# Fused mask, scale and maximum in three attentions, paired reciprocals, and half of the turned probabilities copied by VectorE

## The chip, the cores and the metric

The kernel runs on one core of a Trainium2 chip. The metric is the device time of one execution in microseconds. The core has five engines that run side by side and wait for each other by semaphores: TensorE (PE: matmuls and transposes, with its weight loads as PEld), VectorE (DVE), ScalarE (ACT), GpSimd (POOL) and SyncE (SP, which issues transfers).

## The reference

The reference is a decoder of four layers on x, 8 rows of 256 tokens and 256 features. Each layer has a sequence mixer, an attention over a context and a feed-forward part. The change touches the softmax attentions:

```
_L1_attn   16 heads of 16; relu(q k^T) * R_hat, causal, softmax(scores / 4), times v      (tag L1a)
_L1_xattn  16 heads of 16; score = where(mask == 0, -1e20, q k^T); softmax(score / 4), v  (tag L1x)
_L2_xattn  one head of 256; q k^T / 16 + mask * -1e9; softmax, times v                    (tag L2x)
_L3_xattn  8 heads of 64, 512 keys (256 context + 256 latents); q k^T / 64, masked;
           softmax, times v, Wo, layernorm                                                (tag L3x)
```

## The kernel before, in words

One function, `softmax_attention`, makes L1a, L1x and L3x; `layer2_xattn` makes L2x. Everything is float32. The work of the first is cut into items: 16 per row of the batch, 128 in all. An item is the scores of 128 partitions against W keys: 384 in L1a (a causal tile of 128 and one of 256), two heads' 256 in L1x, 512 keys of one head in L3x. G items are one step: 4 in L1a and L1x (`twins == 2`), 2 in L3x (`twins == 1`). So there are 32 steps in L1a and L1x (4 per row) and 64 in L3x (8 per row). S is the number of softmax rows in an item, 2 in L1a and L1x and 1 in L3x.

An item goes through these stations: TensorE makes the scores in a PSUM bank (`scores`, L1136); VectorE scales them and adds the mask into SBUF (`scale_mask`, L1358; L1355 in L1a) and takes the negated maximum (`maximum`, L1370; L1368 in L1a); ScalarE makes the exponential with that maximum as bias and the sum of the row (`exponent`, L1250; the sum comes out by a second instruction of that line); VectorE inverts the sum (`reciprocal`, L1377); GpSimd multiplies the probabilities by it (L1296; L1300 in L1a); TensorE turns them (`transposes`, L1147) into one of two PSUM banks; ScalarE (L1259) or VectorE (L1346) copies them to SBUF (`take_turned`), after which the bank is free again; TensorE multiplies the values with them (`weigh`, L1169). `by_dve` says which items VectorE copies: the last of each step in L1a and L1x, none in L3x.

Nothing is planned at run time. Each engine's program is written out in order, and each runs its instructions in that order. On TensorE, with LA = 2, step u of the loop is

```
transposes of the first half of step u-2's items
[at the first step of a row: output projection of the row before, L1121]
weigh(u-3)
projections q, k or v of the next row (L1089, L1103, L1110), in most steps
scores(u+1)
transposes of the second half of step u-2's items
```

`weigh` waits until the last two items of its step are copied. VectorE goes item by item: `reciprocal(g - RLAG)` with RLAG = 4 in L1a and L1x and 3 in L3x, then the maximum of item g, with `scale_mask` one item ahead. In L3x `scale_mask(g+1)` of a step's first item stands at the end of the step before, so it is the first thing that VectorE does when new scores are there. Once a row it has also the work of the row's end: in L3x `spread` (statistics of the output, L1388 to L1393) and `output` (normalisation and residual, L1400 to L1413), both ahead of `reciprocal`, in the second and third step after the output projection. ScalarE does, item by item, the exponential and the copy of a turned item.

`layer2_xattn` runs 16 items of 128x256 in the same manner, two per row: copy of the context slice and mask (L1571, L1573), scores (L1508), scale and mask (L1578), maximum (L1581), exponential (L1543), transposes (L1516), copy (L1550), values (L1524), and then reciprocal, scaling and residual on VectorE (L1561 to L1565).

Of the kernel before, what the change touches and what calls it, by code (L numbers as in the profile page):

```python
# [20 lines left out]
B, T, D = 8, 256, 256  # L21
# [12 lines left out]
ACT = mybir.ActivationFunctionType  # L34
ALU = mybir.AluOpType
AX = mybir.AxisListType
# [849 lines left out]
def softmax_attention(c, tag, H, rows, MQ, KT, DV, kind, scale, norm=None):  # L886
# [13 lines left out]
    nc, w = c.nc, c.dram  # L900
    NK, C = KT * P, H * DV
    causal = kind == "decay"
    twins = 2 if rows == 16 else 1
# [4 lines left out]
    G = P // (rows * twins)  # L908
# [5 lines left out]
    n, S = len(items), len(items[0][1])  # L914
# [8 lines left out]
        UNITS = [[("q", 0)], [("q", 1)], [("k", 0)], [], [("v", 0)], [("k", 1)], [("v", 1)], []]  # L923
    in_order = [unit for kind_ in "qkv" for step_units in UNITS for unit in step_units if unit[0] == kind_]
    units_at = lambda u: [(r_, *unit) for r_ in [u // PER_ROW + 1] if r_ < ROWS for unit in UNITS[u % PER_ROW]]
    by_dve = lambda key: twins == 2 and key[0] == "p" and key[1] % G == G - 1

    turned = [(kind_, 0, i) for kind_, i in in_order if kind_ != "k"]
    for u in range(steps + LA):
# [4 lines left out]
    with ExitStack() as stack:  # L934
# [102 lines left out]
        with nc.Fori(0, B // ROWS) as turn:  # L1037
            with nc.Block() as block:
# [169 lines left out]
                def _(act):  # L1208
# [34 lines left out]
                    def exponent(g):  # L1243

                        r, i = divmod(g, n)
                        if g >= NP:
                            act.wait_ge(t_filled, turn_index[("p", g - NP)] + 1)
                        act.wait_ge(sig("max"), g + 1)
                        for e, (t, at, nk) in enumerate(items[i][1]):
                            nc.scalar.activation(p_sb[g % NP][:, at:at + nk], s_sb[g % NSB][:, at:at + nk], ACT.Exp,  # L1250
                                                 bias=nmax[r % 2][:, i, e:e + 1],
                                                 accum_out=rsum[r % 2][:, i, e:e + 1]).then_inc(sig("exp"), 1)

                    def take_turned(j):
# [33 lines left out]
                @block.gpsimd  # L1288
                def _(pool):
                    for r in range(ROWS):  # L1290
                        for i, (h, segs) in enumerate(items):
                            g = r * n + i
                            pool.wait_ge(sig("reciprocal"), g + 1)
                            if len({nk for _, _, nk in segs}) == 1:
                                both = p_sb[g % NP][:].rearrange("p (e s) -> p e s", e=S)
                                last = nc.gpsimd.tensor_tensor(both, both, rsum[r % 2][:, i, :].unsqueeze(2).to_broadcast([P, S, NK]), ALU.mult)  # L1296
                            else:
                                for e, (t, at, nk) in enumerate(segs):
                                    one = p_sb[g % NP][:, at:at + nk]
                                    last = nc.gpsimd.tensor_tensor(one, one, rsum[r % 2][:, i, e:e + 1].to_broadcast([P, nk]), ALU.mult)  # L1300
                            last.then_inc(sig("divided"), 1)

                @block.vector
                def _(dve):
# [8 lines left out]
                    def hide(r):  # L1313

                        if kind == "decay":
                            return
                        dve.wait_ge(sig(f"mask{r % 2}"), 16 * (r // 2 + 1))
                        b_, m_ = bias[r % 2], mask[r % 2]
                        if kind == "pairs":
                            vec.tensor_scalar(b_[:], m_[:], 0.0, -1e20 * scale, ALU.is_equal, ALU.mult).then_inc(sig("bias"), 1)  # L1320
                            dve.wait_ge(sig("bias"), r + 1)
                        if kind == "latent":
                            vec.memset(b_[:, :, T:NK], 0.0)
                            ch.link(vec.tensor_scalar(b_[:, :, 0:T], m_[:], 0.0, -1.0, ALU.not_equal, ALU.add))
                            vec.tensor_scalar(b_[:, :, 0:T], b_[:, :, 0:T], 3e38, None, ALU.mult).then_inc(sig("bias"), 1)
                            dve.wait_ge(sig("bias"), r + 1)
# [21 lines left out]
                    def scale_mask(g):  # L1348
                        r, i = divmod(g, n)
                        bank = s_ring.take(dve)  # L1350
                        if g >= NSB:
                            dve.wait_ge(sig("exp"), S * (g - NSB + 1))
                        s = s_sb[g % NSB]
                        if causal:
                            ins = vec.scalar_tensor_tensor(out=s[:], in0=bank[:, 0:W], scalar=1e-18, in1=rhat[:, items[i][0], :],  # L1355
                                                           op0=ALU.max, op1=ALU.mult)
                        else:
                            ins = vec.scalar_tensor_tensor(out=s[:], in0=bank[:, 0:W], scalar=scale,  # L1358
                                                           in1=bias[r % 2][:].rearrange("p t s -> p (t s)"), op0=ALU.mult, op1=ALU.add)
                        s_ring.empty(ins)  # L1360

                    def maximum(g):
                        r, i = divmod(g, n)
                        dve.wait_ge(s_ring.emptied, g + 1)
                        s, nm = s_sb[g % NSB], nmax[r % 2]
                        if causal:
                            for e, (t, at, nk) in enumerate(items[i][1]):
                                last = vec.tensor_reduce(nm[:, i, e:e + 1], s[:, at:at + nk], AX.X, ALU.max, negate=True)  # L1368
                        else:
                            last = vec.tensor_reduce(nm[:, i, :], s[:].rearrange("p (e s) -> p e s", e=S), AX.X, ALU.max, negate=True)  # L1370
                        last.then_inc(sig("max"), 1)

                    def reciprocal(g):
                        r, i = divmod(g, n)
                        dve.wait_ge(sig("exp"), S * (g + 1))
                        rs = rsum[r % 2][:, i, :]
                        vec.reciprocal(rs, rs).then_inc(sig("reciprocal"), 1)  # L1377

                    proj = out_bank[:].rearrange("p (t d) -> p t d", t=TB)
# [43 lines left out]
                    for g in range(total + (LA + 1) * G):  # L1423
                        r, i = divmod(g, n)
                        u, d = divmod(g, G)
                        if twins == 2:
                            if d == 0 and g < total:
                                scale_mask(g)
                            if d < G - 1 and g < total:
                                scale_mask(g + 1)  # L1430
                            if d == 1 and u > LA:
                                take_turned((u - LA) * G - 1)
                        if i == (G + 2 if twins == 2 else 2) and r + 2 < ROWS:
                            slice_c(r + 2)
                        if i == (2 * G + 3 if twins == 2 else 3) and r + 1 < ROWS:
# [2 lines left out]
                            spread(r - 1)  # L1438
                        if i == ((LA + 2) * G - 1 if twins == 2 else (LA + 3) * G) and 0 < r < ROWS:
                            output(r - 1)  # L1440
                        if RLAG <= g < total + RLAG:
                            reciprocal(g - RLAG)
                        if twins == 1 and g + 1 < total and d < G - 1:
                            scale_mask(g + 1)
                        if g < total:
                            maximum(g)
                        if g + 1 < total and d == G - 1:
                            for r_, what, i_ in units_at(u):
# [20 lines left out]
def layer2_xattn(c):  # L1469
# [4 lines left out]
    with ExitStack() as stack:  # L1474
# [8 lines left out]
        with nc.Fori(0, B // ROWS) as turn:  # L1483
            with nc.Block() as block:
# [44 lines left out]
                def _(act):  # L1529
# [7 lines left out]
                    for i in range(n + 1):  # L1537
                        if i % TB == 0 and i // TB + 1 < ROWS:
                            slice_row(i // TB + 1)
                        if i < n:  # L1540
                            act.wait_ge(sig("max"), i + 1)

                            nc.scalar.activation(prob[i % 3][:], scores[i % 3][:], ACT.Exp, bias=nmax[:, i:i + 1],  # L1543
                                                 accum_out=rsum[:, i:i + 1]).then_inc(sig("exp"), 1)
                        if i >= 1:
                            j = i - 1
                            if j >= 3:
                                act.wait_ge(o_ring.filled, j - 2)
                            bank = t_ring.take(act)
                            t_ring.empty(nc.scalar.activation(probT[j % 3][:], bank[:, 0:T], ACT.Copy))  # L1550

                @block.vector
                def _(dve):
# [13 lines left out]
                    for i, (r, t) in enumerate(items):  # L1567
                        if t == 0:
# [1 line left out]
                                dve.wait_ge(s_ring.filled, TB * (r - 1))  # L1570
                            vec.tensor_copy(cb[r % 2][:], c.ctxT[:, :, bass.ts(row_of(r), T)]).then_inc(sig("sliced_c"), 1)  # L1571
                            dve.wait_ge(sig(f"mask{r % 2}"), 16 * (r // 2 + 1))
                            vec.tensor_scalar(bias[r % 2][:], mask[r % 2][:], -1e9, None, ALU.mult).then_inc(sig("bias"), 1)  # L1573
                            dve.wait_ge(sig("bias"), r + 1)
                        bank = s_ring.take(dve)
                        if i >= 3:
                            dve.wait_ge(sig("exp"), i - 2)
                        s_ring.empty(vec.scalar_tensor_tensor(out=scores[i % 3][:], in0=bank[:, 0:T], scalar=1.0 / 16.0, in1=bias[r % 2][:],  # L1578
                                                              op0=ALU.mult, op1=ALU.add))
                        dve.wait_ge(s_ring.emptied, i + 1)  # L1580
                        vec.tensor_reduce(nmax[:, i:i + 1], scores[i % 3][:], AX.X, ALU.max, negate=True).then_inc(sig("max"), 1)  # L1581
                        if i >= 3:
                            if i >= 5:
                                dve.wait_ge(sig("added"), i - 4)
# [1866 lines left out]
```

## Time and profile before

| | us |
|---|---|
| median of 3 runs | 3799.43 (3787.58 to 3802.03) |
| span of the profiled execution, first to last instruction | 3782.3 |
| PE, PEld busy | 2988.6 (79%), 2137.4 (57%) |
| DVE, ACT, POOL busy | 2358.6 (62%), 1790.9 (47%), 719.5 (19%) |
| mean granted TensorE clock | 0.901 of full |

The profiled execution has no time of its own beside its span; what lies around the span is read as the distance to the median of the runs, 17.1 us. A line with L and a number is the source line of the instruction. "Busy" is the sum over an engine's instructions, and it says nothing about what waits for what: the rows below come from views by time. Clock 1.00 is 2.4 GHz, and 0.50 is 1.2 GHz.

### The profile page before, as it was taken

Reading aid. Unit: us, or ns where it says so; the run is one execution under the profiler, and the core shown is the slowest. Engines: PE = TensorE matmul, PEld = TensorE weight load, DVE = VectorE, ACT = ScalarE, POOL = GpSimd, SP = SyncE. Lnnn points to the kernel's source line nnn. Section 1 sums busy time; section 2 is a strip of 40 time slices with the busy share of each in tenths; the row PEclk is TensorE's granted clock in tenths of the full one; section 3 lists DMA queues with packets and bytes.
Section 4 is the critical chain, followed back from the end, with each engine's and each line's share of the span. In section 5 each row is a group of like instructions: output and inputs, shape, how many; then the busy total and the mean of one; then the engine's idle time right before and its main releaser. Section 6 shows DMA issues by size and latency. Waiting matters only on the chain. (4 is left out here: it accounts for less than half of the span.)

```text
span 3782.3 us, 54983 instructions
## 1 busy us (share of the span) xinstructions
PE 2988.6 (79%) x18517; PEld 2137.4 (57%) x18517; DVE 2358.6 (62%) x5264; ACT 1790.9 (47%) x4260; POOL 719.5 (19%) x833
## 2 busy tenths in 40 slices
PE   6889988998877888377677671596799858888697
PEld 5667766676656567255455331444598435555485
DVE  6776777667566423777678768697511485555423
ACT  6666666666432222577577364402333325556221
POOL 2000000000110322155345100000111002334422
PEclk8999999999989799699899885798799979999798
DMA  3110111011100477000000000000497101000476
GB/s 122 37 34 29 46 37 37 26 48 32 42 4 1 146 248 260 16 2 2 25 10 4 26 0 0 3 0 10 150 349 266 48 25 36 24 24 12 151 256 212
DMA packets 109525, 264.75 MB, mean 70 GB/s; under 512 B 16928, under 2 KB 71456, under 8 KB 104384
## 3 DMA queue, kind: packets, MB, share of 16 engines
q1 hardware_dynamic: 92896, 228.95, 18.1%
q0 software_dynamic: 8688, 23.78, 1.7%
q10 hardware_dynamic: 7664, 8.51, 0.7%
q8 instruction: 152, 2.49, 0.3%
q14 instruction: 125, 1.02, 0.1%
HBM read 213.65 MB, written 47.54 MB: 69 GB/s over the span
## 5 line engine op out<-in xcount | busy, mean ns | idle before, releaser
L3019 POOL TENSOR_TENSOR L0a_sum_sq<-L0a_sum_sq,L0a_sq 128x512 f32<-128x512 f32 x56 | 76.5, 1366 | 890.6 <-ACT L0a_sq L2942 890.6
L1296 POOL TENSOR_TENSOR L3x_p<-L3x_p,L3x_rsum 128x512 f32<-128x512 f32 x128 | 133.0, 1040 | 445.1 <-DVE L3x_rsum L1377 445.1
L3093 DVE SCALAR_TENSOR_TENSOR L0a_xf<-L0a_xc,L0a_conv,L0a_xf 128x256 f32<-128x256 f32 x432 | 191.3, 510 | 21.7 <-ACT L0a_xf L2907 20.4
L2847 ACT ACTIVATE L0a_ex<-bank,L0a_nb 128x128 f32<-128x128 f32 x512 | 144.7, 368 | 96.8 <-PE bank L2776 96.2
L3102 DVE TENSOR_TENSOR L0a_ru<-bank,L0a_um 128x512 f32<-128x512 f32 x128 | 88.0, 687 | 155.4 <-PE bank L2768 150.2
L1358 DVE SCALAR_TENSOR_TENSOR L3x_s<-bank,L3x_bias 128x512 f32<-128x512 f32 x128 | 86.3, 680 | 131.0 <-PE bank L1136 131.0
L1986 PE MATMUL bank<-L2a_half,L2a_diag 128*128 128x512 f32 x328 | 144.1, 601 | 28.4 <-ACT L2a_diag L1969 28.4
L2692 PE MATMUL bank<-x_feat,L0a_wx 128*128 128x256 f32 x576 | 152.4, 414 | 8.2 <-DVE L0a_coef L3178 6.7
L1296 POOL TENSOR_TENSOR L1x_p<-L1x_p,L1x_rsum 128x512 f32<-128x512 f32 x128 | 132.2, 1040 | 135.7 <-DVE L1x_rsum L1377 135.7
L1300 POOL TENSOR_TENSOR L1a_p<-L1a_p,L1a_rsum 128x128 f32<-128x128 f32 (+1 forms) x256 | 123.0, 506 | 135.9 <-DVE L1a_rsum L1377 133.8
L2692 PEld LDWEIGHTS bank<-x_feat,L0a_wx 128*128 128x128 f32 x576 | 113.5, 205 | 36.7 <-DVE L0a_coef L3178 9.2
L2776 PE MATMUL bank<-L0a_ru,L0a_vm 128*128 128x512 f32 x256 | 131.2, 594 | 0.0
L1250 ACT ACTIVATE L1x_p<-L1x_s,L1x_nmax 128x256 f32<-128x256 f32 x256 | 126.8, 500 | 4.6 <-DVE L1x_nmax L1370 4.4
L2733 PE MATMUL bank<-x_feat,L0a_wz 128*128 128x256 f32 x512 | 120.0, 383 | 8.0 <-DVE L0a_far L3083 4.5
L2744 PE MATMUL bank<-L0a_wout,L0a_yzT 128*128 128x256 f32 x512 | 123.7, 397 | 1.0 <-DVE L0a_yzT L3126 1.0
L1986 PEld LDWEIGHTS bank<-L2a_half,L2a_diag 128*128 128x128 f32 x328 | 62.5, 191 | 108.6 <-issue 76.9
L1250 ACT ACTIVATE L3x_p<-L3x_s,L3x_nmax 128x512 f32<-128x512 f32 x128 | 92.0, 719 | 54.7 <-DVE L3x_nmax L1370 54.6
L1250 ACT ACTIVATE L1a_p<-L1a_s,L1a_nmax 128x128 f32<-128x128 f32 (+1 forms) x256 | 113.0, 446 | 3.5 <-DVE L1a_nmax L1368 3.5
L1147 PE MATMUL bank<-ident,L1x_p 128*128 128x128 f32 x512 | 77.5, 286 | 46.8 <-DVE L1x_pT L1346 37.1
L2744 PEld LDWEIGHTS bank<-L0a_wout,L0a_yzT 128*128 128x128 f32 x512 | 101.4, 201 | 18.8 <-issue 4.6
L1705 PE MATMUL bank<-L1f_wT_down,L1f_gate 128*128 128x256 f32 x192 | 44.6, 398 | 85.2 <-DVEq L1868 85.2
L246 ACT ACT_TABLE_LOAD x6 | 7.7, 1283 | 217.9 <-PEq L57 217.9
(738 smaller groups left out, 8243.5 us busy)
## 6 DMA issues: line engine op xcount, KB each, us to landing
L2f_wt<-in_L2f_w SPq DMA_DIRECT2D x23, 2180.0 KB, 9.5
L0f_wt<-in_L0f_w SPq DMA_DIRECT2D x39, 898.0 KB, 6.1
L3f_wt<-in_L3f_w SPq DMA_DIRECT2D x39, 768.0 KB, 5.4
L0a_wx<-in_L0a_wx SPq DMA_DIRECT2D x72, 256.0 KB, 3.1
L0a_wz<-in_L0a_wz SPq DMA_DIRECT2D x32, 512.0 KB, 4.3
context_keys_values<-L2f_zeros ACTq DMA_DIRECT2D x32, 256.0 KB, 4.7
L0f_xs<-rows_by_expert SPq DMA_DIRECT2D x39, 128.5 KB, 3.3
L3f_xs<-rows_by_expert SPq DMA_DIRECT2D x39, 128.5 KB, 2.7
```

The source lines that it names most:

```text
L1250: nc.scalar.activation(p_sb[g % NP][:, at:at + nk], s_sb[g % NSB][:, at:at + nk], ACT.Exp, bias=nmax[r % 2][:, i, e:e + 1], accum_out=rsum ...
L1296: last = nc.gpsimd.tensor_tensor(both, both, rsum[r % 2][:, i, :].unsqueeze(2).to_broadcast([P, S, NK]), ALU.mult)
L1300: last = nc.gpsimd.tensor_tensor(one, one, rsum[r % 2][:, i, e:e + 1].to_broadcast([P, nk]), ALU.mult)
L1358: ins = vec.scalar_tensor_tensor(out=s[:], in0=bank[:, 0:W], scalar=scale, in1=bias[r % 2][:].rearrange("p t s -> p (t s)"), op0=ALU.mult, ...
L1986: last = nc.tensor.matmul((odd_banks(k) if i == 1 else both_banks(k))[q][:], diag[:, k, n, :], moved(i, k, j)[:, q * 4:(q + 1) * 4, :], st ...
L2692: last = mm(bank[:, j * T:(j + 1) * T], wx[q % 3][:, k, j * P:(j + 1) * P], x(k), start=(k == 0), stop=(k == KD - 1))
L2733: last = mm(bank[:, d * T:(d + 1) * T], wz[b % 2][:, k, i * P:(i + 1) * P], x(k), start=(k == 0), stop=(k == KD - 1))
L2744: last = mm(bank[:, t * D:(t + 1) * D], yzT[:, g % NY, t * P:(t + 1) * P], wout[:, g % NPH, :], start=(d == 0), stop=(d == GRP - 1))
L2776: rs.fill(mm(bank[:], vm[:], ru[g % 2][:].rearrange("p j t -> p (j t)"), start=True, stop=True))
L2847: last = a(ex[g % 3][:, j, b * P:(b + 1) * P], bank[:, at:at + P], ACT.Exp, bias=nb[r % 2][:, b, h:h + 1])
L3093: vec.scalar_tensor_tensor(out=xf[q % 4][:, j, :], in0=xc[q % 3][:, j, i:i + T], scalar=conv[:, 2 * p + j, i:i + 1], in1=xf[q % 4][:, j, : ...
L3102: ins = vec.tensor_tensor(ru[g % 2][:], bank[:].rearrange("p (j t) -> p j t", j=2), um[:].unsqueeze(1).to_broadcast([P, 2, T]), ALU.mult)
```

## The change

In L1x, L3x and L2x one VectorE instruction takes the place of the two that scale and mask and that take the maximum. It writes `-scale * (scores + mask)` and the minimum of that, so that ScalarE's exponential now has scale -1. L1x needs two of them per item, since each softmax row has its own minimum. ScalarE waits for that instruction and no longer for a maximum. L1a keeps its two stations.

In L1a, L1x and L3x one reciprocal covers two items; it is issued only at every second item, and GpSimd waits for the pair. In L1x VectorE copies the second turned item of each step as well as the fourth; in L3x it copies the second of two.

```
-    by_dve = lambda key: twins == 2 and key[0] == "p" and key[1] % G == G - 1
+    by_dve = lambda key: key[0] == "p" and key[1] % G in ((G - 1,) if causal or twins == 1 else (1, G - 1))
...
-                        act.wait_ge(sig("max"), g + 1)
+                        act.wait_ge(sig("max") if causal else s_ring.emptied, g + 1)
...
-                                                 bias=nmax[r % 2][:, i, e:e + 1],
+                                                 bias=nmax[r % 2][:, i, e:e + 1], scale=1.0 if causal else -1.0,
...
-                            pool.wait_ge(sig("reciprocal"), g + 1)
+                            pool.wait_ge(sig("reciprocal"), g // 2 + 1)
...
-                            ins = vec.scalar_tensor_tensor(out=s[:], in0=bank[:, 0:W], scalar=scale,
-                                                           in1=bias[r % 2][:].rearrange("p t s -> p (t s)"), op0=ALU.mult, op1=ALU.add)
+                            for e, (t, at, nk) in enumerate(items[i][1]):
+                                ins = vec.tensor_tensor_reduce(out=s[:, at:at + nk], in0=bank[:, at:at + nk], in1=bias[r % 2][:, e, :],
+                                                               scale=-scale, scalar=3e38, op0=ALU.add, op1=ALU.min,
+                                                               accum_out=nmax[r % 2][:, i, e:e + 1])
...
-                        rs = rsum[r % 2][:, i, :]
+                        rs = rsum[r % 2][:, i - 1:i + 1, :]
...
+                            if d == 2 and not causal and LA <= u < steps + LA:
+                                take_turned((u - LA) * G + 1)
...
-                        if RLAG <= g < total + RLAG:
+                        if RLAG <= g < total + RLAG and (g - RLAG) % 2 == 1:
                             reciprocal(g - RLAG)
                         if twins == 1 and g + 1 < total and d < G - 1:
                             scale_mask(g + 1)
-                        if g < total:
+                        if twins == 1 and d == 0 and u > LA:
+                            take_turned((u - LA) * G - 1)
+                        if causal and g < total:
                             maximum(g)
...
-                        s_ring.empty(vec.scalar_tensor_tensor(out=scores[i % 3][:], in0=bank[:, 0:T], scalar=1.0 / 16.0, in1=bias[r % 2][:],
-                                                              op0=ALU.mult, op1=ALU.add))
-                        dve.wait_ge(s_ring.emptied, i + 1)
-                        vec.tensor_reduce(nmax[:, i:i + 1], scores[i % 3][:], AX.X, ALU.max, negate=True).then_inc(sig("max"), 1)
+                        s_ring.empty(vec.tensor_tensor_reduce(out=scores[i % 3][:], in0=bank[:, 0:T], in1=bias[r % 2][:], scale=-1.0 / 16.0,
+                                                              scalar=3e38, op0=ALU.add, op1=ALU.min, accum_out=nmax[:, i:i + 1]))
```

The masks lose their factor `scale` to match (L1x -1e20, L2x -16e9).

## Rows read from the trace of the kernel before

**Rows 1.** Windows of L1x and L3x: length, then busy us (instructions) by engine, clock, DMA.

```profile
1843.00:2107.00 264.00, 211.19 (x1768) 138.21 (x1768) 210.04 (x458) 193.41 (x660) 132.18 (x128) 0.96 0.02 6
3136.00:3500.00 364.00, 317.98 (x2191) 205.20 (x2191) 209.82 (x496) 213.19 (x458) 132.96 (x128) 0.99 0.06 19
```

**Rows 2.** Waits in L3x: engine and line, what for, us in total, times, longest.

```profile
PE bank L1169 <- ACT L3x_pT L1259: 26.8, 57, 0.8
```

**Rows 3.** Timeline of one L3x step without and one with a projection: start, us, engine, [idle before].

```profile
3310.75 1.13 PE L1136 MATMUL bank<-L3x_kT,L3x_qT 64*128 64x512 f32 x4
...
3311.81 1.09 PE L1147 MATMUL bank<-ident,L3x_p 128*128 128x128 f32 x8
3311.91 0.69 DVE L1358 SCALAR_TENSOR_TENSOR L3x_s<-bank,L3x_bias 128x512 f32<-128x512 f32 x1 [0.98 <-PE bank L1136]
...
3312.52 0.15 DVE L1377 RECIPROCAL L3x_rsum<-L3x_rsum 128x1 f32<-128x1 f32 x1
...
3312.75 1.04 POOL L1296 TENSOR_TENSOR L3x_p<-L3x_p,L3x_rsum 128x512 f32<-128x512 f32 x1 [1.29 <-DVE L3x_rsum L1377]
...
3313.30 1.09 PE L1169 MATMUL bank<-L3x_pT,L3x_v 128*64 128x128 f32 x16 [0.40 <-ACT L3x_pT L1259]
...
3314.33 1.99 PE L1089 MATMUL bank<-L3x_xb,L3x_wq 128*128 128x256 f32 x8
...
3316.25 1.13 PE L1136 MATMUL bank<-L3x_kT,L3x_qT 64*128 64x512 f32 x4
```

**Rows 4.** Timeline, start of L3x: the one transpose that waits for GpSimd.

```profile
3143.11 1.04 POOL L1296 TENSOR_TENSOR L3x_p<-L3x_p,L3x_rsum 128x512 f32<-128x512 f32 x1 [228.30 <-DVE L3x_rsum L1377]
...
3144.29 0.63 PE L1147 MATMUL bank<-ident,L3x_p 128*128 128x128 f32 x4 [1.15 <-POOL L3x_p L1296]
```

**Rows 5.** Timeline, L3x: scores and output projection of a row's end, and the last projection.

```profile
3327.26 1.13 PE L1136 MATMUL bank<-L3x_kT,L3x_qT 64*128 64x512 f32 x4
...
3331.30 5.38 PE L1121 MATMUL bank<-L3x_wo,L3x_cT 128*128 128x256 f32 x16 [1.89 <-ACT L3x_cT L1236]
...
3498.77 3.69 PE L1121 MATMUL bank<-L3x_wo,L3x_cT 128*128 128x256 f32 x16 [1.27 <-ACT L3x_cT L1236]
```

**Rows 6.** Timeline, L3x: the two steps with `spread` and with `output` on VectorE.

```profile
3290.79 0.69 DVE L1358 SCALAR_TENSOR_TENSOR L3x_s<-bank,L3x_bias 128x512 f32<-128x512 f32 x1 [7.78 <-PE bank L1136]
...
3292.54 0.16 DVE L1377 RECIPROCAL L3x_rsum<-L3x_rsum 128x1 f32<-128x1 f32 x1
...
3295.12 1.13 PE L1136 MATMUL bank<-L3x_kT,L3x_qT 64*128 64x512 f32 x4
...
3296.28 0.69 DVE L1358 SCALAR_TENSOR_TENSOR L3x_s<-bank,L3x_bias 128x512 f32<-128x512 f32 x1 [1.75 <-PE bank L1136]
...
3300.17 0.15 DVE L1377 RECIPROCAL L3x_rsum<-L3x_rsum 128x1 f32<-128x1 f32 x1
...
3301.31 1.13 PE L1136 MATMUL bank<-L3x_kT,L3x_qT 64*128 64x512 f32 x4
```

**Rows 7.** Timeline of one L1x step.

```profile
1969.61 1.29 DVE L1358 SCALAR_TENSOR_TENSOR L1x_s<-bank,L1x_bias 128x512 f32<-128x512 f32 x2 [1.54 <-PE bank L1136]
...
1972.07 0.68 DVE L1346 COPY L1x_pT<-bank 128x512 f32<-128x512 f32 x1
...
1972.81 0.66 PE L1147 MATMUL bank<-ident,L1x_p 128*128 128x128 f32 x4 [1.22 <-DVE L1x_pT L1346]
...
1973.39 1.07 PE L1169 MATMUL bank<-L1x_pT,L1x_v 128*32 128x256 f32 x16
```

**Rows 8.** By tile: the two-input VectorE form at 256, ScalarE's accumulator read; ns min/median/max.

```profile
L1578 DVE SCALAR_TENSOR_TENSOR L2x_scores<-bank,L2x_bias x16: 414/424/425, 2621.9 to 2664.3; 128x256 f32<-128x256 f32 x16
...
L1250 ACT ACTIVATION_READ_ACCUMULATOR L1x_p<-L1x_s,L1x_nmax x256: 185/192/205, 1846.8 to 2097.5; 128x1 f32 x128
```

**Rows 9.** Timelines: L2x's reciprocal behind TensorE; L1a's transpose behind VectorE's copy.

```profile
2645.79 0.17 DVE L1561 RECIPROCAL L2x_rsum<-L2x_rsum 128x1 f32<-128x1 f32 x1 [0.22 <-PE bank L1524]
...
1655.93 0.55 PE L1147 MATMUL bank<-ident,L1a_p 128*128 128x128 f32 x3 [0.94 <-DVE L1a_pT L1346]
```

More of the change, by code:

```diff
@@ L1319, in hide @@
                         if kind == "pairs":
-                            vec.tensor_scalar(b_[:], m_[:], 0.0, -1e20 * scale, ALU.is_equal, ALU.mult).then_inc(sig("bias"), 1)
+                            vec.tensor_scalar(b_[:], m_[:], 0.0, -1e20, ALU.is_equal, ALU.mult).then_inc(sig("bias"), 1)
                             dve.wait_ge(sig("bias"), r + 1)
@@ L1365, in maximum @@
                         s, nm = s_sb[g % NSB], nmax[r % 2]
[L1366 to L1370, printed above, removed]
+                        for e, (t, at, nk) in enumerate(items[i][1]):
+                            last = vec.tensor_reduce(nm[:, i, e:e + 1], s[:, at:at + nk], AX.X, ALU.max, negate=True)
                         last.then_inc(sig("max"), 1)
@@ L1540, in _ @@
                         if i < n:
-                            act.wait_ge(sig("max"), i + 1)
-                            nc.scalar.activation(prob[i % 3][:], scores[i % 3][:], ACT.Exp, bias=nmax[:, i:i + 1],
+                            act.wait_ge(s_ring.emptied, i + 1)
+                            nc.scalar.activation(prob[i % 3][:], scores[i % 3][:], ACT.Exp, bias=nmax[:, i:i + 1], scale=-1.0,
                                                  accum_out=rsum[:, i:i + 1]).then_inc(sig("exp"), 1)
@@ L1572, in _ @@
                             dve.wait_ge(sig(f"mask{r % 2}"), 16 * (r // 2 + 1))
-                            vec.tensor_scalar(bias[r % 2][:], mask[r % 2][:], -1e9, None, ALU.mult).then_inc(sig("bias"), 1)
+                            vec.tensor_scalar(bias[r % 2][:], mask[r % 2][:], -16e9, None, ALU.mult).then_inc(sig("bias"), 1)
                             dve.wait_ge(sig("bias"), r + 1)
```

## The prediction

> **What bounds the kernel now.** The busy shares name no engine, so I read windows of the changed stages first, then who waits there, then the timeline of one step. In the windows [rows 1] L3x takes 364 us with TensorE busy 318 of them and VectorE only 210; L1x takes 264 us with TensorE and VectorE both near 211. So L3x has VectorE time to spare, and taking work off VectorE brings nothing there unless TensorE waits for that work.
>
> In L3x, TensorE's wait in its steady steps is 0.40 us ahead of `weigh`, for ScalarE's copy of the turned item [rows 2, 3]; it adds to 26.8 us. The reader is to see the period in rows 3: scores at 3310.75, transposes of two items at 3311.81, `weigh` at 3313.30, next work at 3314.33, so 3.58 us from scores to what follows, and 1.92 us more (3314.33 to 3316.25) where a projection stands between. VectorE's first instruction on the new scores starts 1.16 us after the scores began (3311.91), the reciprocal 0.61 later (3312.52), GpSimd's product 0.23 after that.
>
> In L1x the wait is another one [rows 7]: the second transpose of a step stands 1.22 us for its PSUM bank, which VectorE's copy empties. That copy is behind three scale-and-mask instructions, a maximum and a reciprocal, 2.46 us from 1969.61 to 1972.07. Here VectorE's order is on the path. L1a has the same form with 0.94 us [rows 9].
>
> **The paired reciprocal in L3x.** Follow the items. Scores of step u hold items 2u and 2u+1. On TensorE after scores(u) stand the transposes of item 2u-5, then of item 2u-4, `weigh`, a projection, scores(u+1). Before, the reciprocal of item 2u-4 was issued at g = 2u-1, ahead of `scale_mask(2u)`, so a step early; only 2u-3 came at g = 2u, and its transpose was a step away. After, reciprocals are issued only where g - 3 is odd, so at even g: the pair (2u-4, 2u-3) comes at g = 2u. `scale_mask(2u)` was put at the end of g = 2u-1, ahead of it, and waits for scores(u). So the transpose of item 2u-4 now waits for scores(u), through VectorE's fused instruction, the reciprocal and GpSimd's product. That closes a loop over four engines which was open before. The added wait holds all of TensorE, since `weigh`, projection and scores(u+1) are queued behind the transpose, and VectorE, ScalarE and GpSimd wait for scores(u+1).
>
> The new period, from scores to what follows `weigh`: scores until VectorE starts 1.16; fused instruction 0.69 (below); reciprocal until GpSimd starts 0.23; product 1.04 [rows 3]; product until the transpose starts 0.14 (3143.11 + 1.04 to 3144.29, the one place where a transpose waits for GpSimd [rows 4]); four transposes until `weigh` 0.58 (1972.81 to 1973.39 [rows 7]); `weigh` until the next work 1.03 [rows 3]. Sum 4.87 us against 3.58, so 1.29 us more, with a projection or without.
>
> How often: TensorE's loop has such a period for u = 3 to 62, 60 in all.
> - 7 of them hold the output projection. There, scores to projection took 4.04 us, with 1.89 of wait for ScalarE's copy of the context [rows 5]; ScalarE, relieved of a copy that it had to wait for, will be earlier, and the new 3.84 us (the sum without `weigh`) hides what is left: 7 x -0.20 = -1.4 us.
> - 7 hold `spread` between the fused instruction and the reciprocal: 1.75 us in place of 0.61 from the one to the other (3290.79 to 3292.54 [rows 6]), so 1.29 + 1.14 = 2.43 each, 17.0 us. Before, this delayed nothing that was late.
> - 7 hold `output` there, 3.89 us in place of 0.61 (3296.28 to 3300.17). Before, scores to scores took 6.19 us (3295.12 to 3301.31 [rows 6]); after, 4.87 + 3.28 + 1.92 = 10.07. Each +3.88, together 27.2 us.
> - The other 39: 39 x 1.29 = 50.3 us.
>
> Together +93.1 us. I put the first and last steps at nothing: the first transpose waited for GpSimd anyway [rows 4], and at the end no scores are awaited.
>
> **The clock.** After 1.89 us of wait the 16 matmuls of the output projection took 5.38 us, and the same 16 took 3.69 us at the stage's end after 1.27 us [rows 5]; I read the first as run partly at the lower of the clock's two levels. In the 7 steps with `output` TensorE will now stand about 4.9 us; I put `weigh` and projection, 2.95 us, at the same ratio of 1.46, so +1.35 x 7 = 9 us. In the others it stands 1.65 us, near the 1.89, but L1x with 1.22 us in each step keeps 0.96 [rows 1, 7]: I take nothing, and keep 20 such losses of 1.69 us, 34 us, for the upper end.
>
> **The fused instruction.** No row shows one. Its nearest is the two-input instruction: 0.61 us to the next at 512 elements [rows 3], and at 256 a duration of 0.42 [rows 8] less the 0.08 by which neighbours overlap (0.69 - 0.61), so 0.34. It also writes a minimum. ScalarE, which writes a sum, spends a second instruction of 0.19 us on it [rows 8]; a reciprocal of one or two elements on VectorE is 0.15 long [rows 3], and such short ones overlap their neighbours by half. Bounds are 0 and 0.19, and I take 0.08: 0.69 at 512 and 0.42 at 256. The Trainium skill says the same of VectorE (VectorE: DVE Perf Modes, Two Vector instructions with no wait between them): an op that writes out its accumulator is two instructions. By that rule the lower bound falls away; no run shows it for VectorE yet.
>
> In L3x only one fused instruction stands in the loop, so both bounds move the sum by -5 to +7 us. What it removes, a maximum of 0.67 us per item, comes behind the reciprocal and was not waited for.
>
> **L3x, copy by VectorE.** The copy of item 2u-5 is now behind two fused instructions and the reciprocal: 1.16 + 0.69 + 0.08 + 0.69 + 0.68, done 3.30 us after scores(u) began. `weigh` will start at 3.84, so it is hidden. If the GpSimd hold were not there, `weigh` would wait for it, at 3.40 in place of 2.55 (3313.30 - 3310.75 [rows 3]).
>
> **L1x.** RLAG is 4 and a step has 4 items, so the pairs come at the second and fourth item of the next step, still a step of some 8 us ahead of their transposes: no hold. The path to the bank becomes six fused instructions of 256 in place of 2.46 us: 6 x 0.42 = 2.52, +0.06. It counts in 25 of 32 steps (in the 7 with the output projection TensorE waits for ScalarE anyway), so +1.5 us; with the bounds 2.04 and 3.18, -10.5 to +18. The second copy by VectorE lies behind the first bank's release, and hides in the rest of the step.
>
> **L1a and L2x.** L1a loses one reciprocal ahead of the copy in some 24 steps, 0 to 0.15 each; I take -2 us. L2x loses 16 maxima of 0.42 us at most (-6.7 us), but its reciprocal waits for TensorE's last product already [rows 9], behind which only the residual and the next context slice follow; I take -1 us. The paired reciprocals elsewhere save VectorE time that nobody waits for.
>
> **Sum.** 93.1 + 9 + 1.5 - 2 - 1 = +100.6 us on the profiled span of 3782.3, so 3882.9. The runs' median lies 17.1 us above the span; 3900.0 us.
>
> **Rivals.**
> - *The copy alone holds.* If GpSimd's product came in time after all, `weigh` waits for VectorE's copy, 0.85 us per period in 53 periods, +45 us: 3845. For it: only the copy is new to VectorE's order; against: the reciprocal's count. 10%.
> - *The clock falls in most steps.* Up to 60 losses of 1.69 us instead of 7 of 1.35, +92 more: near 3990. For it: 1.65 us stands beside 1.89; against: L1x at 0.96. 8%.
> - *Faster: VectorE's instructions were what TensorE waited for.* It decides where the product of item 2u-4 is there when its transpose's turn comes, 0.45 us after VectorE started on the scores; the chain ahead needs 2.10. Then L3x loses its wait of 26.8 and the 7 x 1.89 for ScalarE, L1x 10.5, L2x 6.7, L1a 2: -59, so 3740. The Trainium skill leans this way (VectorE: DVE Perf Modes, Rules for kernel authors): keep the number of ops low, and restructure a `tensor_reduce` on the hot path; in L3x the trace disagrees, since no engine waits long for the 128 maxima. 7%.
> - *It does nothing of weight*, gains in L1x and L2x paying for a shorter hold: 3%, about 3800.
>
> The forecast itself has 72%. Its own range, with all small bounds, is 3862 to 3955; as nearly all the rest lies below or far above, I give 3860 to 3945. About 0.5% (19 us) can be told from no change: slower 0.90, same 0.03, faster 0.07.
>
> **What would show it.** In L3x a wait of TensorE's transposes for GpSimd's product (L1147 on L3x_p) of about 1.65 us in nearly every step, near 100 us in all, where before there was one of 1.15; the window of L3x near 465 us; GpSimd's products in pairs; about 4.9 us of wait once a row. L1x within 10 us of 264. The forecast is wrong if that wait is absent or if scores follow each other in 3.6 us as before; if L1x grows by 30 us, the fused instruction is dearer than bounded.

## The result and the profile after

| | us |
|---|---|
| before, median of 4 runs | 3794.59 (3787.58 to 3802.03) |
| after, median of 4 runs | 3875.24 (3860.55 to 3879.01) |
| ratio after to before, 95% interval | 1.0216 (1.0186 to 1.0246) |
| span of the profiled execution, before and after | 3782.3 and 3871.7 |
| mean granted clock, before and after | 0.901 and 0.897 |

The kernel became slower, by 80.7 us in the medians and 89.4 us in the spans. I cut both traces into stages, each from VectorE's first instruction on scores to the end of its last residual:

| stage | before | after | difference |
|---|---|---|---|
| L1a | 229.8 | 230.1 | +0.3 |
| L1x | 264.6 | 246.2 | -18.4 |
| L2x | 47.7 | 47.1 | -0.6 |
| L3x | 370.2 | 474.4 | +104.2 |

The sum, +85.5 us, is nearly the whole difference of the spans. The windows of L1x and L3x after, with the columns of [rows 1]:

```profile
1846.00:2092.20 246.20, 201.28 (x1752) 132.93 (x1752) 170.14 (x683) 177.02 (x625) 130.10 (x128) 0.99 0.02 7
3118.70:3593.10 474.40, 341.82 (x2196) 217.22 (x2196) 179.21 (x507) 184.28 (x394) 130.33 (x128) 0.94 0.04 14
```

VectorE is 41 us less busy in L1x (211.16 before) and 35 less in L3x (214.24 before), as the change intends. In L3x that buys nothing: the stage is 104 us longer, and TensorE stands idle for 133 of its 474 us. TensorE's waits name the cause (columns as in [rows 2]); the first line is one that stood there once, with 1.15 us, before the change [rows 4]:

```profile
PE bank L1147 <- POOL L3x_p L1296: 124.4, 62, 4.8
...
PE bank L1147 <- DVE L1x_pT L1346: 26.1, 29, 1.1
...
PE bank L1121 <- ACT L3x_cT L1236: 1.3, 1, 1.3
```

A plain step of L3x after, to be laid beside [rows 3]:

```profile
3338.12 1.13 PE L1136 MATMUL bank<-L3x_kT,L3x_qT 64*128 64x512 f32 x4
...
3339.18 0.66 PE L1147 MATMUL bank<-ident,L3x_p 128*128 128x128 f32 x4
3339.28 0.69 DVE L1359 CUSTOM_DVE_ANT_0 L3x_s<-bank,L3x_bias 128x512 f32<-128x512 f32 x1 [4.72 <-PE bank L1136]
...
3339.90 0.08 DVE L1359 DVE_READ_ACCUMULATOR2_ANT L3x_nmax<- 128x1 f32 x1
3339.90 0.16 DVE L1378 RECIPROCAL L3x_rsum<-L3x_rsum 128x2 f32<-128x2 f32 x1
...
3340.14 2.04 POOL L1296 TENSOR_TENSOR L3x_p<-L3x_p,L3x_rsum 128x512 f32<-128x512 f32 x2 [4.66 <-DVE L3x_rsum L1378]
...
3341.32 0.63 PE L1147 MATMUL bank<-ident,L3x_p 128*128 128x128 f32 x4 [1.49 <-POOL L3x_p L1296]
...
3341.88 1.09 PE L1169 MATMUL bank<-L3x_pT,L3x_v 128*64 128x128 f32 x16
...
3342.91 1.13 PE L1136 MATMUL bank<-L3x_kT,L3x_qT 64*128 64x512 f32 x4
```

The loop reads straight down: scores, fused instruction, reciprocal, GpSimd's products in pairs (one row, x2), TensorE's transpose 0.14 us behind the first of the two and after 1.49 us of wait, values, next scores. From scores to scores it takes 4.79 us. The step with `output` on VectorE, once a row, is the worst:

```profile
3318.98 1.13 PE L1136 MATMUL bank<-L3x_kT,L3x_qT 64*128 64x512 f32 x4
...
3320.14 0.69 DVE L1359 CUSTOM_DVE_ANT_0 L3x_s<-bank,L3x_bias 128x512 f32<-128x512 f32 x1 [6.07 <-PE bank L1136]
...
3324.05 0.16 DVE L1378 RECIPROCAL L3x_rsum<-L3x_rsum 128x2 f32<-128x2 f32 x1
...
3325.47 1.09 PE L1147 MATMUL bank<-ident,L3x_p 128*128 128x128 f32 x4 [4.77 <-POOL L3x_p L1296]
...
3326.49 1.98 PE L1169 MATMUL bank<-L3x_pT,L3x_v 128*64 128x128 f32 x16
...
3328.40 3.10 PE L1103 MATMUL bank<-L3x_xb,L3x_wk 128*128 128x256 f32 x8
...
3331.43 1.13 PE L1136 MATMUL bank<-L3x_kT,L3x_qT 64*128 64x512 f32 x4
```

Between fused instruction and reciprocal now lies all of `output` (3320.14 to 3324.05), TensorE stands 4.77 us, and the work behind the wait runs at the lower clock: four transposes take 1.09 us instead of 0.63, `weigh` 1.98 instead of 1.09, and from 3326.10 to 3331.60 the granted clock is 0.58.

In the steps with `spread` the transposes wait 2.63 us. Two of them, for two rows of the batch, show that behind the same wait the work can run at full speed or not:

```profile
3375.71 1.09 PE L1147 MATMUL bank<-ident,L3x_p 128*128 128x128 f32 x4 [2.63 <-POOL L3x_p L1296]
3376.73 1.98 PE L1169 MATMUL bank<-L3x_pT,L3x_v 128*64 128x128 f32 x16
3378.64 3.57 PE L1110 MATMUL bank<-L3x_wv,L3x_xb 128*128 128x512 f32 x4
...
3438.00 0.63 PE L1147 MATMUL bank<-ident,L3x_p 128*128 128x128 f32 x4 [2.63 <-POOL L3x_p L1296]
3438.56 1.09 PE L1169 MATMUL bank<-L3x_pT,L3x_v 128*64 128x128 f32 x16
3439.58 1.98 PE L1110 MATMUL bank<-L3x_wv,L3x_xb 128*128 128x512 f32 x4
```

The instruction that the trace of before could not show, from L1x:

```profile
1959.20 0.42 DVE L1359 CUSTOM_DVE_ANT_0 L1x_s<-bank,L1x_bias 128x256 f32<-128x256 f32 x1
...
1959.54 0.08 DVE L1359 DVE_READ_ACCUMULATOR2_ANT L1x_nmax<- 128x1 f32 x1
1959.54 0.42 DVE L1359 CUSTOM_DVE_ANT_0 L1x_s<-bank,L1x_bias 128x256 f32<-128x256 f32 x1
1959.89 0.08 DVE L1359 DVE_READ_ACCUMULATOR2_ANT L1x_nmax<- 128x1 f32 x1
1959.89 0.42 DVE L1359 CUSTOM_DVE_ANT_0 L1x_s<-bank,L1x_bias 128x256 f32<-128x256 f32 x1
```

The accumulator read has a row of its own, 0.08 us, but the next instruction starts with it, 0.34 or 0.35 us after the one before. No time of the queue goes to it here.

### The profile page after: what moved, and what is told of

Read it like the earlier page. It is cut to its first block and busy times, and to the rows that moved or that the text cites. A ratio compares the mean times of both kernels' runs of the same rounds, so it can differ in the third digit from the quotient of the medians.

```text
span 3871.7 us, 55038 instructions
## 1 busy us (share of the span) xinstructions
PE 3008.8 (78%) x18517; PEld 2147.9 (55%) x18517; DVE 2271.1 (59%) x5424; ACT 1746.1 (45%) x4164; POOL 713.2 (18%) x833
## 5 line engine op out<-in xcount | busy, mean ns | idle before, releaser
L1359 DVE CUSTOM_DVE_ANT_0 L3x_s<-bank,L3x_bias 128x512 f32<-128x512 f32 x128 | 87.1, 681 | 218.8 <-PE bank L1136 218.8
L1147 PE MATMUL bank<-ident,L3x_p 128*128 128x128 f32 x512 | 86.9, 296 | 124.4 <-POOL L3x_p L1296 124.4
L1147 PEld LDWEIGHTS bank<-ident,L3x_p 128*128 128x128 f32 x512 | 57.0, 147 | 184.9 <-issue 165.2
L1359 DVE CUSTOM_DVE_ANT_0 L1x_s<-bank,L1x_bias 128x256 f32<-128x256 f32 x256 | 92.2, 417 | 38.5 <-PE bank L1136 38.5
L2747 PEld LDWEIGHTS bank<-L0a_wout,L0a_yzT 128*128 128x128 f32 x512 | 102.1, 203 | 19.1 <-issue 4.7
```

The source lines that it names most:

```text
L1147: last = nc.tensor.transpose(bank[:, to * P:(to + 1) * P], p_sb[j % NP][:, b * P:(b + 1) * P], c.ident[:])
L1359: ins = vec.tensor_tensor_reduce(out=s[:, at:at + nk], in0=bank[:, at:at + nk], in1=bias[r % 2][:, e, :], scale=-scale, scalar=3e38, op0=A ...
L2747: last = mm(bank[:, t * D:(t + 1) * D], yzT[:, g % NY, t * P:(t + 1) * P], wout[:, g % NPH, :], start=(d == 0), stop=(d == GRP - 1))
```

## The experiments

Four theories stood against each other: the pair's reciprocal closes the loop (hold), VectorE's copy is late (copy), the fused instruction decides, and the clock. All ratios are to the kernel before on the same chip, with their 95% interval. Kernels e1 to e4 ran together, then e5, e6, e8 and e9, and e10 last; so ratios and stages are to be compared, not times. Each edit is shown in its main lines; `...` stands for code that is not printed.

**e1_pairs_alone**: the kernel before, with pairs in L3x and nothing else.

```
-pool.wait_ge(sig("reciprocal"), g + 1)
+pool.wait_ge(sig("reciprocal"), g + 1 if twins == 2 else g // 2 + 1)
...
-if RLAG <= g < total + RLAG:
+if RLAG <= g < total + RLAG and (twins == 2 or (g - RLAG) % 2 == 1):
```

> The kernel before, with one part of the change alone: in L3x one reciprocal covers two items and stands at every even g. Theory 'hold' (the product of a step's first item now waits for this step's scores, through VectorE and GpSimd): scores follow each other at 4.8 us in place of 3.58 and 6.7 in place of 5.50, transposes wait for GpSimd over 100 us in all, L3x 470 to 480 us in place of 370, time 95 to 110 us above before (about 3895). Rival 'copy' (VectorE's copy of the turned item delays the values): that copy is not in this kernel, so within 5 us of before.

Ratio 1.0281 (1.0259 to 1.0303). L3x took 480.4 us, plain steps 4.77. The wait is there in full without fused instruction or copy, and the time lies 105 us above before, as the theory of the hold had it:

```profile
PE bank L1147 <- POOL L3x_p L1296: 123.0, 62, 4.8
```

**e4_copy_act**: after, with the copies of L3x back on ScalarE.

```
-by_dve = ... in ((G - 1,) if causal or twins == 1 else (1, G - 1))
+by_dve = ... twins == 2 and ... in ((G - 1,) if causal else (1, G - 1))
...
-if twins == 1 and d == 0 and u > LA:
-    take_turned((u - LA) * G - 1)
```

> The changed kernel with all turned items of L3x copied by ScalarE as before, pairs where the change has them. 'Hold': periods stay 4.8 us, L3x within 5 us of 474, time within 6 us of the changed kernel (3869 to 3881). 'Copy': L3x falls to about 370, time to about 3773.

Ratio 1.0223 (1.0199 to 1.0246), L3x 479.5 us, the same wait (124.3 us, 62 times). The copy theory falls: without the copy nothing is gained. L3x is even 5 us longer than in after.

**e2_early_pairs**: after, with RLAG 2 in L3x, so that the pair (2u-4, 2u-3) is inverted at g = 2u-1, ahead of the fused instruction that waits for the next scores.

```
-LA, NP, NPT, NSB, RLAG = ... else (2, 6, 4, 4, 3)
+LA, NP, NPT, NSB, RLAG = ... else (2, 6, 4, 4, 2)
```

> The changed kernel with RLAG 2 in place of 3 in L3x: still pairs, but each stands at odd g, ahead of the instruction that waits for the next scores. 'Hold': no transpose waits for GpSimd; what is left is VectorE's copy, behind two fused instructions, so the values start 3.2 us after the scores (2.55 before), periods 4.2 us, and more in the two steps with row work; L3x about 410 us, time about 3811. 'Copy': it was the copy all along, so little changes, L3x stays near 470, within 10 us of the changed kernel.

Ratio 1.0082 (1.0058 to 1.0107), L3x 434.3 us. The wait for GpSimd is 0.6 us in all, and another has taken its place:

```profile
PE bank L1169 <- DVE L3x_pT L1346: 90.7, 57, 4.4
```

That is VectorE's copy, behind two fused instructions, and behind the row work too where there is some. `weigh` starts 3.22 us after scores began (3220.23 to 3223.45) and a plain step takes 4.25. So the copy was a second bound, hidden under the hold. I had expected L3x at about 410 us; the 24 us more lie in the steps with row work, which take 8.8 to 9.0 us with `spread` and 10.9 to 12.1 with `output`.

**e3_early_pairs_act**: both, the early pairs of e2 and no copy by VectorE in L3x (its copy call left out too).

> As the one with RLAG 2, and all turned items of L3x copied by ScalarE as before. 'Hold': periods 3.58 us again, L3x 365 to 370 us, and L1x keeps its 18 us, so about 3773, below the kernel before. 'Copy': the same. A third theory, that the fused instruction itself is dear in L3x: above 380 us there.

Ratio 0.9921 (0.9897 to 0.9944). L3x 364.6 us, plain steps 3.58 as before. TensorE's largest wait is again the one of [rows 2]. With the hold and its substitute gone, what is left of the change is a gain:

```profile
PE bank L1169 <- ACT L3x_pT L1259: 24.4, 56, 0.8
```

e3 and e4 differ in RLAG alone (2 against 3), so this pair shows the hold by itself: 114.9 us of L3x (479.5 to 364.6), ratio 1.0223 to 0.9921. The theory that the fused instruction is dear in L3x falls too.

**e5_ahead_of_row_work**: after, with reciprocal and copy of L3x moved ahead of `spread` and `output`; RLAG stays 3.

```
+if twins == 1 and RLAG <= g < total + RLAG and (g - RLAG) % 2 == 1:
+    reciprocal(g - RLAG)
+if twins == 1 and d == 0 and u > LA:
+    take_turned((u - LA) * G - 1)
 if i == (LA + 2) * G and 0 < r < ROWS and kind == "latent":
     spread(r - 1)
...
```

> The changed kernel (RLAG 3) with the reciprocal and VectorE's copy of L3x put ahead of the row's spread and output and ahead of the second fused instruction. It tells what the row work inside the hold costs, which the prediction put at 17.0 - 9 + 27.2 - 9 us of row work and 9 of clock, 53 - 18 + 9 = 44 us. 'Hold': plain periods stay 4.8 and 6.7 us; the two steps of a row that took 9.0 and 12.5 us on average fall to 6.7, so L3x falls by 7 x (2.3 + 5.8) = 57 us to about 418, time about 0.7% above before. Rival: the long steps are bound by the row work itself (VectorE busy), not by what waits behind it: then they fall by less than 2 us each and the time stays within 15 us of the changed kernel.

Ratio 1.0106 (1.0064 to 1.0149), L3x 423.6 us. Steps with `spread` and `output` take 6.70 us, no more than any step with a projection; plain ones stay at 4.79. That parts the 104 us in two: some 51 are the row work in the loop, with the clock that it cost, and the rest is the loop itself. The rival, that VectorE's row work bounds these steps by itself, falls.

```profile
PE bank L1147 <- POOL L3x_p L1296: 94.0, 62, 2.2
```

**e6_early_pairs_ahead**: e5 and e2 together, the copy still on VectorE.

> As e5 and RLAG 2: pairs at odd g, copy by VectorE right behind the first fused instruction. 'Hold' and 'copy' both out of the way: the copy is done 2.5 us after the scores began, periods 3.6 and 5.5 us; the output step, 10.4 or 8.7 us with ScalarE's copy, about 6.6; L3x near 340 us, time about 1.5% below before. If the copy by VectorE is no gain even so: L3x at 365, time as with ScalarE's copy (0.8% below).

Ratio 0.9891 (0.9854 to 0.9928), L3x 349.6 us, 20.6 less than before. Plain steps take 3.68; the gain lies in those with the output projection, 6.56 us against 8.18 to 10.38 before, 18.9 us in the seven. ScalarE, without one copy in two, has the context ready (1.3 us of wait in all against 13.5), and the projection does not run at the lower clock. I had expected L3x near 340 us; plain steps did not fall under those of before.

**e8_l1x_unfused**: e3, with mask and maximum apart again in L1x alone.

```
+elif kind == "pairs":
+    ins = vec.scalar_tensor_tensor(out=s[:], in0=bank[:, 0:W], scalar=scale, ..., op0=ALU.mult, op1=ALU.add)
...
-if causal and g < total:
+if kind != "latent" and g < total:
     maximum(g)
```

> The kernel with RLAG 2 and ScalarE's copies in L3x (0.8% below before), with scale-and-mask and maximum of L1x apart again, as before; pairs and the second copy by VectorE stay in L1x. If the fusion gave L1x its 18 us: L1x 262 to 265 us, time 16 to 18 us more, about 0.35% below before. Rival (the second copy by VectorE or the paired reciprocals gave them): L1x stays near 247, time unchanged.

Ratio 0.9972 (0.9954 to 0.9991). L1x 268.1 us against e3's 246.2 (I had expected 262 to 265); the other stages stay within 2 us. So L1x's gain is the fusion's. Pairs and second copy without it shorten an ordinary step by 0.06 us (7.81 against 7.87), and the stage as a whole is not shorter than before. The gain has a spread: L1x is the same code in after and in e2 to e6, and took 246.1 to 249.4 us there, by how many output projections ran slow.

**e9_copies_earlier**: e6, and in L1a and L1x VectorE's copy of a step's last item right behind its first two `scale_mask`, in place of d == 1.

```
-if d < G - 1 and g < total:
-    scale_mask(g + 1)
-if d == 1 and u > LA:
-    take_turned((u - LA) * G - 1)
+if d == 0 and g < total:
+    scale_mask(g + 1)
+if d == 0 and u > LA:
+    take_turned((u - LA) * G - 1)
+if 0 < d < G - 1 and g < total:
```

> As e6, and in L1a and L1x VectorE's copy of a step's last turned item stands behind two items' scores in place of three (and ahead of the first maximum in L1a). If that copy is what the second transpose waits for: the wait falls by 0.69 us per step in L1x and 0.9 in L1a; L1x 246 to about 230, L1a 230 to 206 to 215 us, time about 2.5% below before. If TensorE waits for something else there: both within 3 us, time as e6.

Ratio 0.9832 (0.9795 to 0.9868). L1a 216.3, L1x 240.1, where I had expected 206 to 215 and about 230: much of the gain is missing. The bank's wait is nearly gone (L1x 4.4 us against 26.0 in e6), and ordinary steps are 0.6 to 1.0 us shorter, but steps with the output projection are longer, 11.12 against 9.49 in L1x:

```profile
1941.65 3.44 PE L1121 MATMUL bank<-L1x_wo,L1x_cT 128*128 128x256 f32 x8 [1.59 <-ACT L1x_cT L1236]
```

TensorE now arrives earlier and waits for ScalarE's copy of the context, and the eight matmuls behind the wait take 3.44 us instead of 1.97; from 1943.00 to 1944.00 the granted clock is 0.50.

**e10_context_copy_earlier**: e9, with that copy of ScalarE ahead of the exponential of the iteration before, in L1a and L1x.

```
-if step == LA + 1 and 0 < r < ROWS:
+if twins == 1 and step == LA + 1 and 0 < r < ROWS:
     output(r - 1)
...
+if twins == 2 and step == LA and d == G - 1 and 0 < r < ROWS:
+    output(r - 1)
 if twins == 2 and u < steps:
     exponent(u * G + d)
```

> As the kernel with the pairs in an earlier iteration, the reciprocal and copy ahead of the row work and the VectorE copies of L1a and L1x earlier, and besides in L1a and L1x ScalarE's copy of the context (L1x_cT, L1a_cT) is issued ahead of the row work of its iteration's last part instead of at the start of the next iteration. In that earlier kernel TensorE waits 1.6 to 1.7 us for this copy ahead of each output projection, and the projection's eight matmuls then take 3.04 us instead of 1.97. If that wait is what lowers the clock there, both go: output steps 11.12 to about 9.0 us in L1x and 10.26 to about 7.7 in L1a, so L1x from 240.1 to about 225 us and L1a from 216.3 to about 200, in all some 30 us less than that kernel, a ratio of about 0.975 to the kernel before. If the projection's slow matmuls have another cause (or the copy merely waits for the context's own matmuls wherever it stands), the stages stay at 240 and 216 and the ratio at 0.983.

3693.46 us, ratio 0.9723 (0.9710 to 0.9737), the fastest of all. L1a 199.5 us, L1x 220.8. The same place as above, in e10:

```profile
1914.27 0.66 PE L1147 MATMUL bank<-ident,L1x_p 128*128 128x128 f32 x4 [0.15 <-DVE L1x_pT L1348]
1915.02 1.97 PE L1121 MATMUL bank<-L1x_wo,L1x_cT 128*128 128x256 f32 x8
```

By tile, L1x's output projection in e9, then in e10 (ns of one matmul, min/median/max):

```profile
L1121 PE MATMUL bank<-L1x_wo,L1x_cT x64: 379/631/767, 1879.7 to 2075.1; 128*128 128x256 f32 x64
```

```profile
L1121 PE MATMUL bank<-L1x_wo,L1x_cT x64: 379/379/455, 1859.4 to 2037.0; 128*128 128x256 f32 x64
```

The waits for the context fell from 22.8 us (10.9 in L1x, 11.9 in L1a) to 4.0, the two stages by 36.1. What the waits do not account for, some 17 us, goes with matmuls back at full clock. L1x shows a clock of 1.00 here and 0.96 in e9.

## Why the prediction was right, and where it was not

The direction was right, and in L3x the mechanism; the size came out near in part by luck. Forecast were +100.6 us; measured are +89.4 in the spans (3871.7 against 3882.9 forecast) and +80.7 in the medians (3875.24 against 3900.0). In the spans, L3x gave 2.1 us more than its 102.1, the other three stages 17.2 less than their -1.5, and 3.9 us came outside the stages. Step by step:

- **The period.** 4.87 us forecast, 4.79 measured. The fused instruction gives way after 0.61 us, not 0.69: that is the 0.08 that I put on the accumulator read, where the lower bound of 0 was the right one. The 42 ordinary periods, those at the stage's start among them, grew by 45.9 us together (I had 50.3 for 39). I had put the first and last steps at nothing; the first transpose's wait went from 1.15 to 2.19 us, and the stretch behind the last scores grew by 0.8.
- **Output projection.** -1.4 us forecast, -7.2 measured. I took only the wait for ScalarE off. Three of the seven projections before had run slow (5.38 us, [rows 5]) and four at 3.69; after, all seven take 3.62. The three that are back at full speed make 5.1 of the 7.2 us. My reading of rows 5, that 1.89 us of wait bring the clock down and 1.27 do not, was too simple: before, the same 1.89 us also stood ahead of projections at full speed:

```profile
3190.66 3.69 PE L1121 MATMUL bank<-L3x_wo,L3x_cT 128*128 128x256 f32 x16 [1.89 <-ACT L3x_cT L1236]
...
3283.29 5.38 PE L1121 MATMUL bank<-L3x_wo,L3x_cT 128*128 128x256 f32 x16 [1.89 <-ACT L3x_cT L1236]
```

- **`spread`**: +17.0 forecast, +23.6 measured. The six steps with a projection took 7.84 to 10.78 us, the seventh, without, 5.93. Where transposes, `weigh` and projection run at full speed the step takes 7.84, so `spread` itself costs 16.4 us over the seven, as forecast. The other 7.1 are the clock, in four of the seven (the first of the two shown above loses 2.94 us: 0.46, 0.89 and 1.59), and I had put nothing there.
- **`output`**: +27.2 and 9 for the clock forecast, +41.2 measured together, about 25 and 16. The slowed work is `weigh` and the projection, as I had it, and the transposes too: 1.98 + 3.10 + 1.09 us against 1.09 + 1.99 + 0.63 is 2.46 lost, where I took 1.35 without the transposes and at a ratio read from a projection that was slow only in part. This is a mis-sized term.
- **L3x together.** These four make +103.4 us against my 102.1: errors of -4.4, -5.8, +6.6 and +5.0 cancel, and that is luck.
- **The clock as a rival.** It did not fall in most steps: plain steps keep full speed behind 1.49 us of wait. In the steps with row work it cost some 23 us of the 104, where I had 9.
- **The copy.** Hidden, as said (e4). What I said of it beyond the hold, `weigh` at 3.40 us, came as 3.22 in e2. I had not said that the row work would then lie ahead of the copy as well.
- **The maxima.** I wrote that no engine waits long for them in L3x. That was misread: before, ScalarE stood 54.6 us in all for them, 50 times. But it was not TensorE's path. Without a maximum, in e3, TensorE's wait for ScalarE's copy is 24.4 us against 26.8, so the conclusion holds.
- **L1x.** This step failed: +1.5 us forecast, -18.4 measured. I wrote that the path to the bank becomes 6 x 0.42 = 2.52 us; it became 2.07 (six distances of 0.34 to 0.35), against 2.46. Three things make up the difference. Ordinary steps lose 0.38 us each, 8.0 us in 21 of them (7.87, 8.13, 7.00 became 7.49, 7.75, 6.63). Of the six steps with the output projection that have scores behind them, three went from 11.12 to 9.49, -4.9 us in all. Their waits are the same in sum as before (1.22 + 0.52 and 0.84 + 0.90), as I had said; only the clock differs, and why is open. And from the first scores to the fifth, where scores waited for VectorE to empty their banks, it is 5.6 us less (24.4 to 18.8), which I had not looked at; part of it again is matmuls that no longer run slow. My lower bound of -10.5 us covers the first alone.
- **L1a and L2x.** +0.3 and -0.6 against -2 and -1: nothing, as good as.
- **The distance of 17.1 us.** Here the reading was wrong. The run of the changed kernel whose span is the profiled one took 3873.53 us at 3871.7, so 1.8 us lie around the span, and so it is in every run whose span is known (1.7 to 1.9). The rest of the 17.1, 15.3 us, was how far the profiled execution of before lay under the median. Here the median lies 3.5 above the span.

The terms outside L3x came to -18.7 us, against my -1.5. Without the hold, as in e3, that makes the change a gain.

## What to carry to other kernels

When an instruction is made rarer by serving two items at once, ask when the *first* of the two is now served, and what stands ahead of it in its engine's order: one that waits for the next round's input turns slack into a loop over all engines, and any long work between costs its whole length (in e5, with that work moved out, L3x is 51 us shorter). One repair keeps the pairing and puts it one item earlier, ahead of the instruction that waits: e4 at 1.0223 against e3 at 0.9921, which differ in nothing else. Undoing the pairing in the changed kernel was not run, and no run shows that the pairing gains anything in L3x: plain steps take 3.58 us both in before and in e3. And after each bound that goes, look for the wait that replaces it: here GpSimd's product, VectorE's copy, ScalarE's context copy, in turn.

## What the runs showed of the hardware

- VectorE's fused add, scale and minimum with an accumulator costs no more than the two-input instruction without one: 0.42 us at 256 and 0.69 at 512 elements, as long as the other at both sizes, and 0.34 to 0.35 and 0.60 to 0.62 from start to start (the other: 0.61 at 512). The Trainium skill (VectorE: DVE Perf Modes, Two Vector instructions with no wait between them) says that such an op is two instructions; the trace agrees, with a row of 0.08 us, but that row takes no time from the queue.
- The length of a wait is not its whole price. Behind 1.59 us of it (e9) eight matmuls took 3.44 us; with the wait gone (e10), 1.97. One matmul takes 379 ns or, where the granted clock is 0.50, up to 767.
- What decides whether the clock falls behind a given wait stays open. The same wait goes both ways: in L3x, 1.89 us left a projection at 3.69 us or at 5.38 (before), and 2.63 us left the work behind it at full speed in three steps and not in four (after). In after's L1x, 0.90 us left four projections at 1.97 and one at 3.04. At the two ends, in after, 1.49 us in each plain step of L3x never brought it down, and 4.77 us did in all seven steps with `output`. Nor is the wait just ahead of an instruction the only one that counts: in e1 three of L3x's output projections took 5.38 us though almost none of their wait for ScalarE was left; what stood in these steps was the 1.47 us for GpSimd, ahead of the transposes.
